# Transpose copies moved from VectorE to ScalarE, and a normalisation step moved from VectorE to GpSimd, in a transformer layer on eight cores

## The reference

```
x = x + linear_attention(layernorm(x))        # 16 heads, phi(x) = elu(x) + 1, Wq Wk Wv Wo
h = layernorm(x)
h = h + mla(rmsnorm(h))                       # causal softmax attention, latent width 512, 16 heads
h = h + moe(rmsnorm(h))                       # 8 experts of width 2048, top 2, silu
x = x + h
```

## Time and profile before

| | us |
|---|---|
| runs shown: median of 2 | 3642.17 |
| runs shown: lowest, highest | 3539.47, 3744.86 |
| the profiled execution's own time | 3549.59 |
| its span (slowest core, core 7) | 3548.0 |
| spans of the eight cores | 3508.7 to 3548.0 |
| mean granted TensorE clock of the cores | 0.881 to 0.886 |
| busy: PE, DVE, ACT, POOL | 2792.6, 787.5, 758.2, 364.5 |

### The profile page before, as it was taken

How to read it: one execution, slowest core, us unless ns; L and a number is a source line. 1 busy time by engine, 2 the same in 40 slices (tenths; PEclk the granted TensorE clock), 3 DMA queues, 4 the chain that set the end, 5 groups by cost and what they waited for, 6 DMA issues and landing times.

```text
span 3548.0 us, 37239 instructions; the slowest of 8 cores (3508.7 to 3548.0 us)
## 1 busy us (share of the span) xinstructions
PE 2792.6 (79%) x14080; PEld 1242.3 (35%) x14080; DVE 787.5 (22%) x1600; ACT 758.2 (21%) x860; POOL 364.5 (10%) x375
## 2 busy tenths in 40 slices
PE   2778454975556656658989989999999999999997
PEld 1333222432222222223434434444444344444433
DVE  3126445264332232230011011001100110011011
ACT  4112000112434526621101110111011011101110
POOL 0114000000000010021101110110011001101110
PEclk9788776975666668879999999999999999999999
DMA  8001003010000000036443642662364436524641
GB/s 181 1 1 26 0 1 48 1 24 1 1 1 1 1 1 1 1 44 64 45 63 36 72 52 23 69 72 24 48 72 44 66 33 71 63 24 57 72 80 51
DMA packets 297854, 135.98 MB, mean 38 GB/s; under 512 B 268880, under 2 KB 269904, under 8 KB 297680
## 3 DMA queue, kind: packets, MB, share of 16 engines
q0 software_dynamic: 292432, 116.69, 29.0%
q1 hardware_dynamic: 5248, 16.91, 1.4%
HBM read 241.73 MB, written 8.39 MB: 70 GB/s over the span
## 4 chain that ended last, share of the span: by engine, by line
PE 68%; DVE 13%; ACT 7%; DMA 6%; issue 5%; DVEq 1%; ACTq 0%; POOL 0%; another core or an unknown queue 0%; SPq 0%; POOLq 0%
PE PS L977 25%; PE PSQ L949 23%; ACT PTb L738 5%; PE PSQ L290 4%; DMA WSb<-w 4%; PE PSQ L727 3%; DVE PTb L748 3%; DVE accT L987 2%; PE PSQ L404 2%; PE PS L710 2%; PE PST L202 2%; PE PS L797 2%; PE PSQ L359 2%; PE PSQ L568 2%; DMA accT<-x 1%
## 5 line engine op out<-in xcount | busy, mean ns | idle before, releaser
L949 PE MATMUL PSQ<-N,WSb 128*128 128x512 bf16 x4096 | 906.9, 384 | 53.0 <-DMA WSb<-w 52.6
L977 PE MATMUL PS<-N 128*128 128x512 bf16 x2816 | 628.4, 379 | 60.4 <-DVE accT L987 60.4
L958 ACT ACTIVATE N<-PSQ 128x1024 bf16<-128x1024 f32 x256 | 262.4, 1025 | 1625.2 <-PE PSQ L949 1625.1
L949 PEld LDWEIGHTS PSQ<-N,WSb 128*128 128x128 bf16 x4096 | 404.7, 99 | 552.3 <-issue 82.2
L987 DVE SCALAR_TENSOR_TENSOR accT<-PS,gts,accT 128x512 f32<-128x512 f32 x256 | 192.1, 750 | 1759.8 <-PE PS L977 1745.8
L977 PEld LDWEIGHTS PS<-N 128*128 128x128 bf16 x2816 | 270.5, 98 | 408.9 <-issue 92.9
L738 ACT ACTIVATE PTb<-PSQ 128x1024 bf16<-128x1024 f32 x320 | 328.0, 1025 | 224.4 <-PE PSQ L727 208.3
L151 POOL DMA_DIRECT2D WSb<-w x256 | 223.8, 874 | 1229.6 <-PE PSQ L949 1229.6
L977 PE MATMUL PS<-A,N 128*128 128x512 bf16 x1280 | 289.2, 379 | 36.4 <-DVE accT L987 36.4
L710 PE MATMUL PS<-N,PTb 128*128 128x65 bf16 x2176 | 148.2, 219 | 209.0 <-DVE PTb L748 155.8
L727 PE MATMUL PSQ<-qpad,N 128*128 128x512 bf16 x640 | 265.3, 529 | 3.5 <-DVE qpad L672 3.5
(11 more groups left out here) (131 smaller groups left out, 1195.3 us busy)
## 6 DMA issues: line engine op xcount, KB each, us to landing
WSb<-w POOLq DMA_DIRECT2D x256, 256.0 KB, 4.8
N<-w POOLq DMA_DIRECT2D x11, 2048.0 KB, 16.7
A<-w POOLq DMA_DIRECT2D x5, 2048.0 KB, 15.5
accT<-x SPq DMA_DIRECT2D x4, 2048.0 KB, 31.2
out<-accT SPq DMA_DIRECT2D x2, 4096.0 KB, 12.8
N<-aWk POOLq DMA_DIRECT2D x1, 2048.0 KB, 33.0
N<-aWv POOLq DMA_DIRECT2D x1, 2048.0 KB, 54.6
A<-aWq POOLq DMA_DIRECT2D x1, 2048.0 KB, 67.2
```

Source lines behind the costliest of these rows:

```text
L949: st=(kc == 0), sp=(kc == KD - 1): e_.matmul(out=QB[bb], lhsT=w1slot[sl][:, kk * 128:(kk + 1) * 128], rhs=N1v[:, kk, g * 1024 + hf * 512:g ...
L958: tsl = b.emit("s", lambda e_, mm=m: e_.activation(out=N2a[:, mm * 1024:(mm + 1) * 1024], in_=PSQ.ap()[:, (mm % 2) * 1024:(mm % 2) * 1024 ...
L977: st=(kh == 0), sp=(kh == KH - 1): e_.matmul(out=YEB[pp][:, 0:512], lhsT=N2a[:, kk * 1024 + t_ * 128:kk * 1024 + t_ * 128 + 128], rhs=w2a[ ...
```

## The change

Three edits.

- `transpose_tile` gets an argument `eng`. With `"s"` the copy out of `PST` is an ACT instruction (`activation` with `Copy`) instead of a DVE `tensor_copy`. It is given in `emit_a4_tail` (16 copies), in stage 3 (16 copies), and in both places of the tails (16 and 16 copies). The 16 copies of stage 1 stay on DVE.
- In the tails the layer norm of `accT` (L803) is issued by POOL instead of DVE. For each tile both halves stand ahead of the tile's matmuls in the source, and on POOL's list ahead of the tile's two additions to `accT`. They wait for the last reader of `scrF` in the tile before (`last_zstt`), for its last sum of squares (`last_tsq`), and once for the statistics (`tok_b1c`).
- DVE's addition (L807, L818 in the changed file) now waits for the matmuls and for POOL's half. The separate wait for `tok_accg` goes.

```diff
-    def transpose_tile(src16, dst_ap, waits):
+    def transpose_tile(src16, dst_ap, waits, eng="v"):
...
-        b.wait("v", tok)
-        ev = b.emit("v", lambda e, d=dst_ap: e.tensor_copy(out=d, in_=PSTr), inc="v")
+        b.wait(eng, tok)
+        if eng == "v":
+            ev = b.emit("v", lambda e, d=dst_ap: e.tensor_copy(out=d, in_=PSTr), inc="v")
+        else:
+            ev = b.emit("s", lambda e, d=dst_ap: e.activation(out=d, in_=PSTr, func=AF.Copy), inc="s")
         bank_free[6] = ev
...
-        ev, _ = transpose_tile(attn, afm_r, attn_toks)
+        ev, _ = transpose_tile(attn, afm_r, attn_toks, eng="s")
...
-            ev, mm = transpose_tile(*pend_tr[0:3])
+            ev, mm = transpose_tile(*pend_tr[0:3], eng="s")
...
-            ev, _ = transpose_tile(ms, ms.rearrange("p (k n) -> p k n", n=128), av_evac_toks)
+            ev, _ = transpose_tile(ms, ms.rearrange("p (k n) -> p k n", n=128), av_evac_toks, eng="s")
...
+            tgc2 = [None, None]
+            for half in range(2):
+                b.wait("g", last_tsq[0])
+                b.wait("g", last_zstt[0])
+                if tok_b1c[0] is not None:
+                    b.wait("g", tok_b1c[0])
+                tgc2[half] = b.emit("g", lambda e, a=acc_t, hf=half, tt=qt: e.tensor_scalar(
+                    out=scrF.ap()[:, hf * 512:(hf + 1) * 512], in0=a[:, hf * 512:(hf + 1) * 512],
+                    scalar1=stats.ap()[:, 16 + tt:17 + tt], scalar2=stats.ap()[:, 32 + tt:33 + tt],
+                    op0=ALU.subtract, op1=ALU.mult), inc="g")
...
-                b.wait("v", tw)
-                b.wait("v", tok_accg[0])
-                b.emit("v", lambda e, a=acc_t, hf=half, tt=qt: e.tensor_scalar(
-                    out=scrF.ap()[:, hf * 512:(hf + 1) * 512], in0=a[:, hf * 512:(hf + 1) * 512],
-                    scalar1=stats.ap()[:, 16 + tt:17 + tt], scalar2=stats.ap()[:, 32 + tt:33 + tt],
-                    op0=ALU.subtract, op1=ALU.mult))
+                b.waits("v", [tw, tgc2[half]])
...
+            last_zstt[0] = tzt
...
-            zev, zmm = transpose_tile(ms, N1v[:, 0:8, qt * 128:(qt + 1) * 128], [ztoks[qj]])
+            zev, zmm = transpose_tile(ms, N1v[:, 0:8, qt * 128:(qt + 1) * 128], [ztoks[qj]], eng="s")
```

More of the change, by code:

```diff
@@ L440, in emit_b1_chain @@
         b.emit("v", lambda e: e.reciprocal(out=st[:, 0:16], in_=st[:, 0:16]))
-        b.emit("v", lambda e: e.tensor_mul(out=st[:, 0:16], in0=st[:, 0:16], in1=st[:, 32:48]))
+        tok_b1c[0] = b.emit("v", lambda e: e.tensor_mul(out=st[:, 0:16], in0=st[:, 0:16], in1=st[:, 32:48]), inc="v")
     b1_tsq = None
+    tok_b1c = [None]
     NUMB = {4: SB[0], 5: SB[1], 7: S7}
@@ L658, in build @@
     tok_accg = [None]
+    last_tsq = [b1_tsq]
+    last_zstt = [None]
     tok_av_final = None
@@ L821, in build @@
                 b.wait("v", tsq)
+                last_tsq[0] = tsq
             tms = b.emit("v", lambda e: e.tensor_add(out=st[:, 0:1], in0=st[:, 0:1], in1=st[:, 1:2]), inc="v")
```

## The result

The changed kernel's median is 3582.14 us over 11 runs (3566.55 to 3850.72), that of the kernel before, run beside it, 3546.11 over 10 (3531.86 to 3918.91). The ratio is 1.0085, 95% interval 1.0062 to 1.0108: +0.85%, some 30 us slower. The profiled execution took 3569.3 us, its slowest core (core 1) 3567.7.

A forecast was written before the change was run, and what follows sets the result against it. Turns between engines, none of them full, were taken to bound the changed stages. Stage 2 +9, stage 3 +3.6 and tails -7.8 gave +4.8 on 3549.59, so 3554 us; its own range 3535 to 3580, the whole range 3530 to 3650.

The forecast's parts named there:

- What bounds the changed stages: Stages 2, 3 and tails: engines take turns, none is full; each edit is priced by what it adds to a turn.
- The price of one copy: Any copy PE waits for: ACT instead of DVE costs +0.24 us, bounds -0.10 and +0.34.
- Stage 2: 16 copies there: +3.8 us direct, contained in +10.2 from four lost clock rises instead of one; +9 taken, bounds 0 and +17.
- The copies in the tails: Tails: first-part copies cost +2.9 us; in third parts an earlier first copy gains 1.55, three cost 0.24 each, together -3.3.
- the price d of POOL's normalisation: Tails: time POOL needs to normalise one half, taken as 0.9 us, with 0.61 and 1.26 also priced.
- The term for 12 halves: Tails, first halves of tiles 2 to 4: POOL starts behind scrF's last reader, +0.47 us each, +5.6 in all.
- the tails' sum: Four tails: 2.9 - 13.0 + 5.6 - 3.3 = -7.8 us, bounds -13 and -2.
- The clock in the tails: Tails: changes of PE's clock, not in the sum; rivals put them at -22 us if gained, +18 if lost.
- POOL does not deliver early: Tails: POOL's normalisation is stretched or costs 1.26 us or more, 12 first halves lose 0.84 or more; 3559 us, chance 0.11.
- Clock gained: Tails: shorter pauses keep PE's clock up, 20 halves gain 22 us; whole kernel 3527 us, chance 0.10.
- Lateness absorbed: Stage 2: late tiles run more matmuls at the high clock, pitch stays 13.65, cost 0; whole kernel 3545 us, chance 0.17.
- Clock lost: Stage 2 and tails: added pauses keep PE at the low clock, +34 and +18 us; whole kernel 3601 us, chance 0.09.

The follow-up runs named there:

- the pair at clock 0.99: Kernel before plus 28 unread matmuls a tile in stage 2, its copies on DVE or ACT: stage 2 192.4 or 197.1 us, ratio 0.9944 or 0.9971.

## Why the prediction was right or wrong

- **What bounds the changed stages** was right: turns between engines. The added matmuls, which shorten no turn but in its matmul part, took 30 us from stage 2. Taking work off DVE gained only where that work had stood in a turn and its replacement was ready in time (20 halves, 12 us); elsewhere it gained nothing.
- **The price of one copy**, 1.03 - 0.69 - 0.10 = +0.24, was close. ACT's bf16 copy takes 1.02, as the fp32 one did. The earlier start of 0.10 did not recur, as the upper bound allowed. In stage 3 it is 4.6 / 15 = 0.31, and 4.6 stands where 3.6 was forecast. The rule that ScalarE is closer to PSUM (Trainium skill, Advanced Engine Details and Errata, section TRN2 Errata) would have had the copies gain; ACT's 1.02 against DVE's 0.69 shows that it does not carry that far here.
- **Stage 2** was right in size (+9 forecast, +9.5) and in mechanism: 4.7 direct, the rest lost clock, shown by the pair at clock 0.99. Four long groups instead of one were forecast, and four came on every core.
- **The copies in the tails.** In the first parts they cost 3.8 where 2.9 was forecast (the part grew from 6.93 to 7.88). In the third parts the mechanism was right, the first copy starts behind the root and gains 1.4 of the forecast 1.55, but the next three cost 0.38 each instead of 0.24: four tails gain 1.0, not 3.3. A third part as a whole, from the end of the last matmul with Wo, shortened from 13.72 to 12.81; 0.65 of this 0.91 is the normalisation that no longer stands there, so that its nearness to the forecast 0.8 is chance.
- **The failed step is the price d of POOL's normalisation**, "I take 0.9", with 0.61 and 1.26 as its ends. It measures 2.07. The term for 12 halves was +5.6 and is +20.6. With it the tails' sum would have been 2.9 - 13.0 + 20.6 - 3.3 = +7.2 instead of -7.8, and the whole +20. The ends were rows of other operations on the same engine. Each was cheaper by its kind, and nothing in the trace of before said that a scalar operation costs more than a two-tensor one. An end of a range taken from another operation is no bound. The figure of 769 ns for a single-input loop (Trainium skill, GPSIMD Engine Reference, section Performance versus the Vector engine) lies further off still; no run here shows it, and the single-input operations measured were 0.61, 1.50 and 2.08. The page's advice to keep elementwise work on VectorE agrees with the prices here, 0.55 on DVE against 2.07, though the 20 halves that had time to spare gained on POOL all the same.
- **The clock in the tails** was left out of the sum and kept for rivals. It is a second, smaller failure, a term put at nothing. The matmuls on the chain took 64.0 instead of 59.3, +4.7; the rest of the tails grew by 10.4, where the normalisation's +7.8 and the copies' 3.8 - 1.0 make 10.6. Together that is the 15.2. The same sum ran from 59.2 to 60.5 in five profiles with unchanged tails, so the 4.7 is known to a us or so; up to half of it may be what stage 2's copies alone do to the tails.
- **Rivals.** "POOL does not deliver early" was the mechanism that came true, priced at 3559 because it too used 1.26. "Clock gained" did not happen: the tails' 256 matmuls took 92.3 instead of 96.0, but it was the 12 groups off the chain that became faster, and the 20 on it became slower. The pause of 1.74 that this rival read as one ahead of a second half stands ahead of the next tile's first half in the earlier trace rows, which for three tiles in four is off the chain. "Lateness absorbed" fell with stage 2. "Clock lost" held in part: in stage 2 as often as the sum said, and in the tails by those 4.7.
- The forecast of no change by the measure of 2% was met; the sum's sign was right, but with 25 of the 30 us missing: its two large terms of opposite sign nearly cancelled, and one rested on an unseen price.

## What to carry to other kernels

In a chain of turns an instruction is worth what it adds to the turn, whatever its engine's load: ask for each moved instruction whether it can start before the turn needs it (20 of these 32 halves could, 12 could not), and move only those. Do not bound an unseen operation by other operations of that engine; time it alone first, in a place where the engine is idle. Before a shorter matmul is counted as a gain, look whether it stands on the chain. Where TensorE's clock falls in pauses that come again and again, added matmuls with no reader are a cheap test of how much the clock costs; here 15 a tile, with one pause left empty, brought stage 2 only to 214.4 and 28 a tile to 192.4, and those in four stages were worth more than the change itself.

## What the runs showed of the hardware that was not expected

- POOL's tensor_scalar with two per-partition scalars, fp32: 1.22, 2.08 and 3.78 us at 256, 512 and 1024 columns; with one constant 1.50 at 512; a copy 0.61; an addition of two tensors 1.26.
- The same instruction took 2.36 instead of 2.07 when DVE's fp32 normalisation in SBUF was under way as it started (96 of 96 in the run with POOL for 20 halves), and DVE's stayed at 0.55. Beside DVE's addition alone it stayed at 2.07 (96 of 96 in the changed kernel).
- A delay of 0.3 a tile cost 4.7 us over sixteen tiles at clock 0.99 and 8.5 to 10 at clock 0.70, with long groups every third or fourth tile on every core.
- The same four tails took 241.6 to 243.0 us in five profiles, but 237.7 to 246.3 on single cores, by which of their matmuls ran at the high clock; in three profiles with nothing different but stage 2's copies on ACT, or these and added matmuls there, they took 244.7 to 246.4.
